# Moving one copy behind the last two masks on VectorE in the second and third attention of an eight-stage transformer kernel

## The reference

```python
x = _layernorm(x + _L1_attn_ref(x, Wq, Wk, Wv, Wo, rel_emb))   # head size 8, rotary, learned bias by distance
...
x = _layernorm(x + _L2_attn_ref(x, Wq, Wk, Wv, Wo))            # head size 16
# each: softmax(causal(q @ k.T * scale + bias)) @ v @ Wo
```

## Time and profile before

| | us |
|---|---|
| median of 3 runs | 2719.86 (2719.12 to 2722.84) |
| profiled execution | 2722.79 |
| its span, first to last instruction | 2721.0 |
| mean granted TensorE clock, share of full speed | 0.943 |

### The profile page before, as it was taken

The page is one execution under the profiler, slowest core; times in us unless marked ns, Lnnn a source line. Parts: engine busy times, 40 slices in busy tenths (PEclk is TensorE's granted clock), DMA queues, the critical chain, the costliest instruction groups (busy, mean ns, idle before and its releaser), DMA issues. The chain is left out here.

```text
span 2721.0 us, 72168 instructions
## 1 busy us (share of the span) xinstructions
PE 2325.5 (85%) x21404; PEld 1819.9 (67%) x21404; DVE 1863.6 (68%) x8093; ACT 1408.3 (52%) x3365; POOL 1357.8 (50%) x1540
## 2 busy tenths in 40 slices
PE   7999998795999925889998889768978999999986
PEld 5777776463666624757776677657766777777755
DVE  4777776563888843568887689856655767777746
ACT  2444444222666613556665466535546666666614
POOL 4778876002666624367776455423324454445501
PEclk8999999897999967999999899989989999999978
DMA  2000000332000014600000100000000000000001
GB/s 75 3 0 0 0 0 0 84 62 99 2 0 0 0 64 132 192 2 1 0 0 2 40 2 0 0 1 2 0 23 1 2 0 0 0 0 0 0 1 32
DMA packets 44039, 55.98 MB, mean 21 GB/s; under 512 B 6800, under 2 KB 29417, under 8 KB 43564
## 3 DMA queue, kind: packets, MB, share of 16 engines
q1 hardware_dynamic: 41580, 49.37, 6.3%
q0 software_dynamic: 2304, 4.79, 0.5%
HBM read 47.11 MB, written 9.74 MB: 21 GB/s over the span
## 5 line engine op out<-in xcount | busy, mean ns | idle before, releaser
L1110 POOL TENSOR_TENSOR a_sm<-a_sm,a_top 128x512 f32<-128x512 f32 x512 | 523.8, 1042 | 201.8 <-DVE a_top L908 199.9
L1033 ACT ACTIVATE a_pr<-a_sm 128x512 f32<-128x512 f32 x512 | 315.6, 628 | 153.6 <-POOL a_sm L1110 114.5
L908 DVE CUSTOM_DVE_ANT_0 a_sm<-bank,cst 128x128 f32<-128x128 f32 (+1 forms) x1024 | 299.9, 353 | 88.7 <-PE bank L770 84.4
L784 PE MATMUL bank<-cst,a_pr 128*128 128x128 f32 x2304 | 311.4, 277 | 0.8 <-ACT a_pt L1043 0.3
L2935 POOL TENSOR_TENSOR a_pr<-a_sm,a_rden 128x512 f32<-128x512 f32 x192 | 197.3, 1049 | 228.2 <-DVE a_rden L2721 227.8
L784 PEld LDWEIGHTS bank<-cst,a_pr 128*128 128x128 f32 x2304 | 258.6, 142 | 34.2 <-issue 23.0
L1043 ACT ACTIVATE a_pt<-bank 128x512 f32<-128x512 f32 x352 | 200.8, 589 | 142.9 <-PE bank L784 140.3
L916 DVE COPY a_pt<-bank 128x512 f32<-128x512 f32 x224 | 153.5, 685 | 60.5 <-PE bank L784 59.3
L804 PEld LDWEIGHTS bank<-a_pt,a_v 128*32 128x32 f32 x4608 | 119.6, 110 | 99.9 <-issue 89.1
L2695 DVE CUSTOM_DVE_ANT_0 a_sm<-bank,cst 128x256 f32<-128x256 f32 (+1 forms) x512 | 149.8, 353 | 52.5 <-PE bank L2579 45.3
L804 PE MATMUL bank<-a_pt,a_v 128*32 128x128 f32 x4608 | 156.5, 276 | 17.8 <-issue 6.8
(11 more groups left out here) (492 smaller groups left out, 5931.0 us busy)
## 6 DMA issues: line engine op xcount, KB each, us to landing
f_w<-in_l_w SPq DMA_DIRECT2D x40, 256.0 KB, 3.4
f_spread<-gate_rows SPq DMA_DIRECT2D x16, 512.0 KB, 6.9
W<-in_l_w SPq DMA_DIRECT2D x2, 2048.0 KB, 9.7
x_sorted<-in_l_blank SPq DMA_DIRECT2D x4, 660.0 KB, 7.0
f_xin<-x_sorted SPq DMA_DIRECT2D x10, 264.0 KB, 3.2
X<-in_x SPq DMA_DIRECT2D x4, 512.0 KB, 7.2
a_bias<-bias_rows SPq DMA_DIRECT2D x1, 2048.0 KB, 7.9
X<-y_rows SPq DMA_DIRECT2D x8, 256.0 KB, 4.7
```

What stands on the lines that cost most here:

```text
L784: mm = pe.transpose(tbank[j % 2][:, c * P:(c + 1) * P], pr[j][:, c * P:(c + 1) * P], ident)
L908: ins = dve.tensor_tensor_reduce(sm[j][:, m * kw:(m + 1) * kw], sbank[j][:, m * kw:(m + 1) * kw], mk, 1.0, 3.0e38, ALU.add, ALU.min, top[: ...
L1033: act.activation(pr[j][:, :], sm[j][:, :], ACT.Exp, scale=-1.0).then_inc(S["probs"], 1)
L1110: pool.tensor_tensor(whole, whole, top[:, qt, a:a + m].unsqueeze(2).to_broadcast([P, m, kw]), ALU.subtract).then_inc(S["shifted"], 1)
```

## The change

The call `copies(i, s, (0, 1))` in VectorE's `slot` moves from between the masks of units 1 and 2 to behind the mask of unit 3:

```diff
             def slot(i, s):
                 if in_loop(i):
                     mask(i, s, 0)
                     mask(i, s, 1)
                     steps_in(i, s, 0)
-                copies(i, s, (0, 1))
-                if in_loop(i):
                     mask(i, s, 2)
                     steps_in(i, s, 1)
                     mask(i, s, 3)
+                copies(i, s, (0, 1))
+                if in_loop(i):
                     if lanes == 2:
                         steps_in(i, s, 2)
```

## The result

The changed kernel takes 2740.16 us (median of 4 runs, 2737.05 to 2745.35) against 2720.26 us before on the same chip: ratio 1.0074, 95% interval 1.0056 to 1.0091, so 20 us slower. Timed once more beside other kernels it is 17.9 us slower (1.0065). The forecast was 2729.4, with a range of 2720 to 2737: the direction is right, the size is half of what came.

A forecast was written before the change was run, and what follows sets the result against it. TensorE was taken to lead, its scores waiting for VectorE's norm. Losses of 0.26 and 0.35 us per sequence, 16 sequences each, made 9.8, about 9.5 with the first slot: 2719.86 + 9.5 = 2729.4 us, range 2720 to 2737.

The forecast's parts named there:

- It adds and removes no instruction: Whole kernel: no instruction or DMA is added or removed; only VectorE's queue is reordered.
- The first is a gain: VectorE, second attention: masks 2, 3 and norm skip the wait; norm up to 0.47 us earlier in quad 2, 0.42 quad 0.
- So a new loop arises: Both attentions: scores, first mask, all masks, copy of unit 1, turn of unit 3, projection, next scores; 5.90 to 6.99 us.
- The sum for the second attention: Quad 2 5.90 against 6.00, quad 0 6.99 against 6.62, quad 1 stays 5.51; 18.40 against 18.14 us per sequence, +0.26.
- the v projection to the next scores, 0.44: Second attention, quad 2: 4 matmuls of 128 columns take 0.44 us, half the 0.87 of 8 such.
- the hand-over: From the end of VectorE's copy to TensorE's turn of unit 3: 0.17 us, with bounds 0.05 and 0.25.
- The third attention, +0.35: Quads 0, 1 and 2 take 6.99, 6.38 and 6.43; 19.80 against 19.45 us per sequence.
- The clock is granted in full in both stretches: TensorE, second and third attention: full clock with present idle times, which grow by about 0.3 us per sequence.
- Sixteen sequences in each stage: Second and third attention: 16 x 0.26 + 16 x 0.35 = 9.8 us, about 9.5 with the first slot.
- Rival A: Both attentions: the norm's wait falls and nothing replaces it; some 1.65 us per sequence, 26 us faster, 2693; chance 0.07.
- Rival B: Both attentions: no measurable change; earlier masks 2 and 3 hasten the values product, 8 us back, +1.5, 2721; chance 0.15.
- Rival C: Both attentions: TensorE's score waits stay beside the new wait at turn 3; 53 us slower, 2773; chance 0.03.

The follow-up runs named there:

- e7_later: Changed kernel with the copy of unit 1 moved further back, behind residual, norm and moments: 2788.10 us, 1.0243 of before.
- e4_mid: Changed kernel with the copy of unit 1 in the middle place, between masks 2 and 3: 2697.52 us, 0.9907 of before; timed again 2700.28.
- e3_proj: Changed kernel with TensorE's projection of the next sequence ahead of the turn of unit 3: 2711.52 us, 0.9961 of before.
- e9_head: Changed kernel with the early copy of before in the slots outside the hardware loop: 2733.24 us, 1.0046 of before.
- e8_q1: Kernel before with the late copy of unit 1 only in quad 1 of the third attention, inside the hardware loop: 2718.78 us, 0.9988 of before.
- e5_proj_before: Kernel before with TensorE's projection ahead of the turn of unit 3: 2737.79 us, 1.0068 of before.
- e6_mid_proj: Changed kernel with the copy of unit 1 between masks 2 and 3 and the projection ahead of turn 3: 2713.19 us, 0.9969 of before.

## Why the prediction was right in direction and wrong in size

- *"It adds and removes no instruction", "The first is a gain"*: right. The norm is no longer waited for.
- *"So a new loop arises"*: right, and shown four ways: by TensorE's waits at line 784; by e7_later, which lengthens the loop and the slots; by e4_mid, which shortens it and gains; by e3_proj, which takes the projection off it and gains 29 to 31 us on top of the change.
- The sum for the second attention, +0.26 per sequence, measured +0.49. Quad 0 was right (6.99, measured 7.05). The mis-sized term is **the v projection to the next scores, 0.44**, "half the 0.87 of 8 such". It measures 793.14-792.60 = 0.54, and 811.83-811.15 = 0.68 in every second sequence, so 0.61 on average: 16 x 0.17 = 2.7 us. The turn of unit 3 behind a gap measures 0.47 for 0.435, which the hand-over takes back (0.14 for 0.17). So quad 2 loses 0.12 on average where 0.10 were to be gained. With quad 0's 0.06 the second attention is 16 x 0.23 = 3.7 us over the sum. Before, the projection's length was hidden in the scores' wait. Every second sequence is also the one at the end of the hardware loop's body, which holds two; whether the loop's jump is the 0.14 us is open: no run separates it, and in the third attention, whose loop ends at the same slot behind a longer projection, that slot takes 6.42 both times.
- The third attention, +0.35, measured +0.44: quad 0 took 7.05 for 6.99 and quad 1 6.42 for 6.38. Sixteen masks took 3.39 for 3.36 (1322.99-1319.60), the first mask came 1.40 for 1.36 behind the scores of quad 1. That is 1.5 us.
- **"The clock is granted in full in both stretches", and "Sixteen sequences in each stage" at the steady rate**: this step failed outright. The stretches were read from 720 and 1190 on and left out the starts, where the clock was already 0.86 over the first 12 us of the third attention. There the late copy costs 3.5 us beyond the steady loss, in the main because the new loop then ran over turn, projection and scores at the lower clock (8.61 us for 6.42): no term of the sum stood for it, and no bound. e9_head, with the early copy in the sequences outside the loop, gives back 4.0 us there.
- Added up: the forecast's 9.5, the second attention's terms 3.7 (the v projection 2.7 of them), the third attention's 1.5 and the start 3.5 give 18.2, where the profiles differ by 18.0. That it fits so closely is in part chance: the first seven slots of the second attention lost 0.3 us, not the 1.1 of the steady rate, and 0.6 us lie outside both attentions.
- Rival A (2693) did not come with this order: the bank took the norm's place. Its gain exists (2697.52 and 2700.28): the middle place frees mask 3 and the norm of the wait and gives the bank back in time. The rule of the Trainium skill that was weighed (Perfetto Trace Analysis, "Optimization Strategy") points at the dependency that ended the wait. The runs agree that an earlier norm gains: 23 to 25 us with the middle place, where the bank is still given back in time; with the change's own order they do not.
- Rival B did not come, but for the reason given, and only for that: its mechanism works (e8_q1), and in the changed kernel the new loop covers it.
- Rival C did not come: the waits for `a_on` are gone.

Open: why the clock came back later with the late order; the cause of e5_proj_before's +16, which is only read from waits (its steady slots give 16 x 0.86 = 13.8, and two single slots took 1.6 us more each); and e6_mid_proj, whose steady slots would give 16 x 0.84 = 13 us less than before where 8.6 was measured.

## What to carry to other kernels

Before an instruction is moved behind others to spare them its wait, write down who waits for what it frees, here a PSUM bank: its latest harmless place is given by that one and its earliest by its input, and the place to try is the first at which the input is just there. Add up the new path with every term measured where it is exposed, as a term hidden under a wait today can be longer than it looks. Read the first sequences of a stage apart from the steady ones, clock included, and give them a term of their own.

## What the runs showed of the hardware

- TensorE's clock at the start of the third attention came back at different times: in the first 12 us of the third attention it was 0.86, 0.72 and 0.70 of full, in the next 12 it was 1.00, 1.00 and 0.87 (before, e9_head, after). A score group takes 1.14 or 1.15 us at the upper level (2.4 GHz) and took 1.99 to 2.09 at the lower (1.2 GHz), in these traces always behind a gap. The gap just before does not decide it: in the changed kernel's second attention the group behind 2.70 us idle took 1.14 and the one behind 1.72 took 2.09.
- A short group costs more than its share: eight turns take 0.87 us to the next group, four take 0.46 to 0.47, and the v projection's four matmuls of 128 columns take 0.54, or 0.68 at the end of the loop's body.
- A PSUM bank passes from VectorE's copy to a TensorE that waits for it in 0.14 us (791.99 to 792.13; at the start of the third attention 1186.97 to 1187.11).
- Medians of before on four occasions were 2720.26, 2722.75, 2721.75 and 2722.96: 2.7 us apart, so kernels are compared with before of their own chip.
